# Attention block with an FP8 layer, one core: values and x transposes in mixed blocks, norm values by sums, spread products, four score banks and an end in halves

## What is computed

```python
def _layernorm(x, axis=-1, eps=1e-05):
    m = jnp.mean(x, axis=axis, keepdims=True)
    v = jnp.var(x, axis=axis, keepdims=True)
    return (x - m) / jnp.sqrt(v + eps)
# x: (16, 512, 256)
def attn(x, qkv_w, qkv_b, proj_w, proj_b):        # on _layernorm(x)
    qkv = jnp.einsum('bsd,ed->bse', x, qkv_w) + qkv_b
    # q, k, v: 16 heads of 16 features
    scores = jnp.einsum('bhqe,bhke->bhqk', q, k) * 16 ** -0.5
    out = jnp.einsum('bhqk,bhke->bhqe', jax.nn.softmax(scores, axis=-1), v)
    return jnp.einsum('bsd,ed->bse', out, proj_w) + proj_b
def ffn(x, weight_fp8, bias, input_scale, weight_scale):   # on _layernorm(x)
    x_q = jnp.clip(x / input_scale, -448.0, 448.0).astype(jnp.float8_e4m3fn)
    x_dq = x_q.astype(x.dtype) * input_scale
    return jnp.einsum('bsi,oi->bso', x_dq, weight_fp8 * weight_scale) + bias
x = x + attn(_layernorm(x), ...)
x = x + ffn(_layernorm(x), ...)
```

## Time and profile before

| | |
|---|---|
| median of 3 runs | 969.15 us (968.81 to 969.47) |
| the profiled execution's own time | 968.59 us |
| its span, first to last instruction | 966.8 us |
| TensorE busy | 930.0 us (96%) |
| VectorE, ScalarE, GpSimd busy | 843.8, 656.4, 515.9 us |
| mean granted TensorE clock | 0.974 of full speed |

### The profile page before, as it was taken

One profiled execution on the slowest core, in us unless ns is written; L12 is line 12 of the kernel. 1 busy time (PEld: TensorE's weight loads), 2 busy tenths in 40 slices (PEclk: granted clock), 3 DMA queues, 4 the chain that ended last, 5 costly groups with the idle time before them and its releaser, 6 DMA issues.

```text
span 966.8 us, 16811 instructions
## 1 busy us (share of the span) xinstructions
PE 930.0 (96%) x5847; PEld 439.4 (45%) x5847; DVE 843.8 (87%) x1264; ACT 656.4 (68%) x1209; POOL 515.9 (53%) x528
## 2 busy tenths in 40 slices
PE   7799999999999999999999999999999999999993
PEld 4343444444444454544444444444444454433342
DVE  5678889898999989898998989899898989989846
ACT  3157777777777777767677776767777776776760
POOL 4522428467373847647383754738285573715222
PEclk9769999999999999999999999999999999999996
DMA  6971635438083554717265472817556280731010
GB/s 174 159 91 44 107 52 99 79 62 138 29 142 53 100 78 77 124 40 140 44 115 64 83 116 50 140 34 128 72 74 105 35 136 10 136 42 35 13 45 23
DMA packets 46350, 79.45 MB, mean 82 GB/s; under 512 B 10104, under 2 KB 13304, under 8 KB 46264
## 3 DMA queue, kind: packets, MB, share of 16 engines
q1 hardware_dynamic: 45976, 77.97, 47.1%
q10 hardware_dynamic: 288, 0.39, 0.3%
HBM read 18.42 MB, written 8.39 MB: 28 GB/s over the span
## 4 chain that ended last, share of the span: by engine, by line
PE 92%; DVE 2%; ACT 2%; SPq 1%; DMA 1%; issue 1%; ACTq 0%; POOL 0%; DVEq 0%; POOLq 0%
PE ps_t L551 29%; PE ps_o L591 26%; PE ps_m L426 10%; PE ps_s L570 8%; PE ps_m L475 5%; PE ps_m L499 5%; PE ps_m L531 3%; PE ps_m L412 1%; ACT pt L709 1%; PE ps_s L483 1%; DMA xin<-in_x 1%; SPq L309 1%; PE ps_m L514 1%; DVE mx L874 0%; PE ps_s L692 0%
## 5 line engine op out<-in xcount | busy, mean ns | idle before, releaser
L709 ACT ACTIVATE pt<-ps_t 128x512 f32<-128x512 f32 x1024 | 558.0, 598 | 213.9 <-PE ps_t L551 210.5
L874 DVE TENSOR_REDUCE mx<-ps_s 128x2 f32<-128x1024 f32 x512 | 615.3, 1209 | 57.4 <-PE ps_s L570 53.7
L551 PE MATMUL ps_t<-qs,ks 50*128 50x512 f32 x1024 | 391.9, 455 | 8.2 <-ACT pt L709 7.9
L570 PE MATMUL ps_s<-ks,qs 48*128 48x512 f32 x1024 | 380.7, 463 | 8.0 <-DVE nmax L923 4.1
L551 PEld LDWEIGHTS ps_t<-qs,ks 50*128 50x128 f32 x1024 | 164.0, 185 | 296.3 <-ACT pt L709 214.0
L591 PE MATMUL ps_o<-pt,vt 128*32 128x512 f32 x2048 | 272.6, 605 | 0.0
L1176 POOL TENSOR_TENSOR on<-ot,rden 128x256 f32<-128x256 f32 x63 | 39.3, 624 | 243.2 <-DVE rden L935 243.2
L570 PEld LDWEIGHTS ps_s<-ks,qs 48*128 48x128 f32 x1024 | 158.4, 188 | 18.9 <-issue 11.8
L426 PE MATMUL ps_m<-xnT_p,wqkv_p 128*128 128x512 f32 x360 | 109.9, 428 | 1.0 <-POOL xnT_p L1145 1.0
L1167 POOL TENSOR_TENSOR parts<-parts 128x512 f32<-128x512 f32 x60 | 81.3, 1356 | 4.9
L591 PEld LDWEIGHTS ps_o<-pt,vt 128*32 128x32 f32 x2048 | 40.4, 108 | 86.1 <-issue 85.1
(11 more groups left out here) (113 smaller groups left out, 763.3 us busy)
## 6 DMA issues: line engine op xcount, KB each, us to landing
qs<-parts SPq DMA_DIRECT2D x186, 128.0 KB, 4.6
ks<-parts SPq DMA_DIRECT2D x186, 128.0 KB, 5.4
xin<-in_x SPq DMA_DIRECT2D x16, 512.0 KB, 3.6
xres<-in_x SPq DMA_DIRECT2D x16, 512.0 KB, 5.8
out<-h SPq DMA_DIRECT2D x31, 256.0 KB, 2.1
qs<-nmax SPq DMA_DIRECT2D x256, 4.0 KB
pt<-in_qkv_wT SPq DMA_DIRECT2D x1, 768.0 KB, 5.2
qs<-parts SPq DMA_DIRECT2D x12, 64.0 KB, 3.6
```

The lines of the kernel that those rows point to most:

```text
L551: nc.tensor.matmul(ps_t[:, g, :], ks[par][rows, slot, keys], qs[par][rows, slot, :], start=True, stop=True).then_inc(st_done, 1)
L570: done = nc.tensor.matmul(ps_s[:, s % 2, g, :], qs[par][rows, slot, queries], ks[par][rows, slot, :], start=True, stop=True)
L709: nc.scalar.activation(pt[n % 2][:, w % 2 + 2 * a, w // 2, :], ps_t[:, a, :], ACT.Exp, scale=SCALE).then_inc(exp_done, 1)
L874: dve.tensor_reduce(mx[:, r, :, s % QUARTER], ps_s[:, s % 2, :, :], AX_X, ALU.max).then_inc(max_done, 1)
```

## The change

- Slots 1 to 15: `project_v` and `transpose_x` are replaced by `values_and_x` at the same four steps 20, 22, 24, 26. Each block has six value products (256 columns, one token group) and two transposes of x (128 columns each) into the other half of the same bank. ScalarE reads each block out with two copies of 256 columns instead of one of 512. In slot 15 the blocks have no transposes.
- The norm values become `tensor_reduce` over columns: `mv1` and `mv2` get a third column that holds eps, so that variance + eps is a sum of two columns, and -mean a negated sum of one. The sums of the first norm move from steps 7, 12, 13, 15 with the end at 17 to 5, 7, 10, 12 with the end at 13, and GpSimd's `layernorm_x` goes ahead of `low_oT` of batch u-2.
- Start: x of batch 2 is loaded first in `first_slot` and summed at the end of VectorE's `prepare`, in front of the first maximum; the bias product moves from `ps_o` to `ps_m`, its addition to `prepare`; the transposes of x for batch 1 and five unread matmuls go ahead of the first scores; ScalarE issues the stack of the last keys; SyncE does the first maximum rows ahead of the stack of batch 1. In slot 1 the query and key products of batch 1 stand one at a time in steps 4 to 15 and three at a time in 16 to 19, and unread matmuls in steps 0 to 3 and 8.
- Slot 17: after its first step the odd steps of `scores_t` use the bank pair `ps_s[0]`, so that each waits for the exponential two steps back. The unread matmuls become one in each of the steps 2, 4, 6, 8. The rounding of batch 14 moves from step 8 to 4, the norm's end from 3 to 2, `out_back` from 6 to 9, `copy_oT` from 8 to 12; GpSimd norms first and adds the FP8 layer's bias after the rounding.
- End: `finish` does all value products first and then turns, divides, copies and projects in halves of 256 columns; the normalization of h moves from VectorE to ScalarE (two activations for each of four token groups); 26 unread matmuls stand behind the last projection.

```diff
-LAST_ROUND = 8
+LAST_ROUND = 4
+LAST_END = 2
+LAST_BACK = 9
+LAST_COPY = 12
+FILL_VALUES = 3
+FILL_NORM = 26
-FILL_STEPS = range(3, 12)
+FILL_STEPS = (2, 4, 6, 8)
...
-PROJECT_QK_1 = ((4,), (6,), (8,), (10, 12))
+PROJECT_QK_1 = (range(4, 10), range(10, 16), (16, 17), (18, 19))
-PROJECT_V = (20, 22)
-TRANSPOSE_X = (24, 26)
-TRANSPOSE_X1 = (0, 2)
+VALUES_AND_X = (20, 22, 24, 26)
-LN1_SUM = (7, 12, 13, 15)
-LN1_END = 17
+LN1_SUM = (5, 7, 10, 12)
+LN1_END = 13
+WARM_SCORES = 5
+WARM_STEPS = (1, 1, 1, 1, 0, 0, 0, 0, 3)
...
+        def t_bank(b, s, g):
+            if b == B - 1 and s > HALF_STEPS and s % 2:
+                return ps_s[:, 0, g, :]
+            return ps_t[:, g, :]
...
             def first_slot():
+                load(2, 0)
                 sp.wait_ge(ones, 1)
...
-                for n in (2, 3):
-                    stack(0, 0, n)
-                load(2, 0)
+                stack(0, 0, 2)
...
-                for half in range(2):
-                    project_v(0, half)
+                for i in range(NJ):
+                    project_values(ps_t[:, i // 2, i % 2 * D:(i % 2 + 1) * D], 0, i)
+                pe.wait_ge(low_ready, 4)
+                pe.wait_ge(v_ready, 4)
+                for i in range(WARM_SCORES):
+                    nc.tensor.matmul(ps_s[:, 1, 1, :], wqkv_p[:, 0, 0, 0:P], wqkv_p[:, 0, 0, 0:S], start=True, stop=True)
+                for c in range(NC):
+                    transpose_x(1, c)
...
+            def values_and_x(u, i):
+                take_bank("values_and_x", i, u)
+                project_values(ps_m[:, 0:D], u, i)
+                if u < B - 1:
+                    c, half = i // 2, i % 2
+                    pe.wait_ge(xn_ready, u + 2)
+                    for j in range(2):
+                        last = nc.tensor.transpose(ps_m[:, D + j * P:D + (j + 1) * P],
+                                                   xn[:, 2 * half + j, c * P:(c + 1) * P], ident[:])
+                    last.then_inc(xt_done, 1)
...
+                if b == B - 1 and s == HALF_STEPS + 1:
+                    pe.wait_ge(max_done, STEPS * b + STEPS - 1)
+                elif b == B - 1 and s > HALF_STEPS:
+                    pe.wait_ge(exp_done, 2 * STEPS * b + 2 * s + g - 3)
+                elif past(2 * STEPS * b + 2 * s + g - 1):
                     pe.wait_ge(exp_done, 2 * STEPS * b + 2 * s + g - 1)
...
             def finish(b):
                 values(b, b % 2, UNITS - 1, 0)
+                values(b, b % 2, UNITS - 1, 1)
                 pe.wait_ge(oT_high, NT * b + 1)
...
+                unread(FILL_VALUES)
+                for half in range(2):
+                    pe.wait_ge(oT_high, NT * b + 2 + half)
+                    project_last(1, half, PAIRS[0:3:2])
+                    pe.wait_ge(oT_low, NT * b + 2 + half)
+                    project_last(1, half, PAIRS[1:2]).then_inc(proj_done, 1)
+                unread(FILL_NORM)
...
-                dve.tensor_scalar(nm1[:], mv1[:, :, 0], -1.0, None, ALU.mult).then_inc(ln1_ready, 1)
-                dve.tensor_scalar(ve1[:], mv1[:, :, 1], EPS, None, ALU.add).then_inc(ln1_ready, 1)
+                dve.tensor_reduce(nm1[:], mv1[:, :, 0:1], AX_X, ALU.add, negate=True).then_inc(ln1_ready, 1)
+                dve.tensor_reduce(ve1[:], mv1[:, :, 1:3], AX_X, ALU.add).then_inc(ln1_ready, 1)
...
+                finish_bias()
+                for j in range(NJ):
+                    ln1_sum(2, 0, j)
+                ln1_finish(2)
```

More of the change, by code:

```diff
@@ L354, in slot @@
                     load(u + 2, par)
+                if u == 1:
+                    rows(0, 0, 0)
                 if present(0):
                     stack(u, par, 0)
-                if present(1):
+                if present(1) and u > 1:
                     rows(u - 1, 1 - par, 0)
@@ L401, in take_bank @@
                     pe.wait_ge(y_ready, 2 * before + m + 1)
+                elif last == "bias":
+                    pe.wait_ge(const_v, 3)
                 bank_user[:] = [name, n, b]
             def transpose_x(u, c):
-                first = u == 0
-                bank = ps_t[:, c, :] if first else ps_m[:]
-                if not first:
+                bank = x_bank(u, c)
+                if u > 1:
                     take_bank("transpose_x", c, u)
+                if u == 1 and c == 1:
+                    pe.wait_ge(v_ready, 2)
                 pe.wait_ge(xn_ready, u + 1)
@@ L550, in scores_t @@
                 rows = slice(HALF * g, HALF * g + KM)
-                nc.tensor.matmul(ps_t[:, g, :], ks[par][rows, slot, keys], qs[par][rows, slot, :],
+                nc.tensor.matmul(t_bank(b, s, g), ks[par][rows, slot, keys], qs[par][rows, slot, :],
                                  start=True, stop=True).then_inc(st_done, 1)
@@ L614, in slot @@
                         transpose_max(u - 1, TRANSPOSE_MAX.index(s))
+                    if u == 1 and s < len(WARM_STEPS):
+                        unread(WARM_STEPS[s])
                     for j in range(2):
@@ L635, in slot @@
                     if u == LAST_SLOT and s in FILL_STEPS:
-                        for i in range(2 - s % 2):
-                            nc.tensor.matmul(ps_s[:, 0, i, :], wqkv_p[:, 0, 0, 0:P], wqkv_p[:, 0, 0, 0:S],
-                                             start=True, stop=True)
+                        pe.wait_ge(nmax_split, 8 * (u - 2) + 8)
+                        nc.tensor.matmul(ps_s[:, 1, 0, :], wqkv_p[:, 0, 0, 0:P], wqkv_p[:, 0, 0, 0:S],
+                                         start=True, stop=True)
                     if s % 2:
@@ L651, in bias, with unread @@
                 for t in range(NT):
[L652 removed]
+                    last = nc.tensor.matmul(ps_m[:, 0:D], b_v_rep[:, t, :], wproj[:, t, :],
                                             start=(t == 0), stop=(t == NT - 1))
                 last.then_inc(bias_done, 1)
[L656 to L665 removed]
+            def unread(count):
+                for i in range(count):
+                    nc.tensor.matmul(ps_t[:, 1, :], wqkv_p[:, 0, 0, 0:P], wqkv_p[:, 0, 0, 0:S], start=True, stop=True)
@@ new lines, in project_last @@
+            def project_last(t, half, picks):
+                for j in range(2):
+                    tok = slice((2 * half + j) * P, (2 * half + j + 1) * P)
+                    for pw, px in picks:
+                        last = nc.tensor.matmul(ps_s[:, half, j, 0:D], oT_p[:, px, t, tok], wproj_p[:, pw, t, :],
+                                                start=(t == 0 and (pw, px) == (0, 0)),
+                                                stop=(t == 1 and px == 1))
+                return last
@@ L1054, in finish @@
                 hb = xin[1]
[L1055 to L1063 removed]
+                blocks = [slice(S // 64 * half, S // 64 * (half + 1)) for half in range(2)]
@@ new lines, in finish, with tokens_out, reciprocal @@
+                columns = [slice(S // 2 * half, S // 2 * (half + 1)) for half in range(2)]
+                def tokens_out(half):
+                    dve.wait_ge(pv_done, UNITS * b + UNITS)
+                    dve.wait_ge(on_ready, 4 * b + 3)
+                    dve.transpose(ot[:, blocks[half]].rearrange("p a c -> p (a c)"),
+                                  ps_o[:, columns[half]]).then_inc(ot_ready, 1)
+                def reciprocal(half):
+                    dve.wait_ge(ot_ready, 4 * b + 4 + half)
+                    dve.reciprocal(rden[:, blocks[half]], ot[:, blocks[half], HD]).then_inc(rden_ready, 1)
@@ new lines, in divide, with heads_back @@
+                def divide(half):
+                    dve.wait_ge(rden_ready, 4 * b + 4 + half)
+                    dve.tensor_tensor(on[:, blocks[half], HD:2 * HD], ot[:, blocks[half], 0:HD],
+                                      rden[:, blocks[half]].unsqueeze(2).to_broadcast([P, S // 64, HD]),
+                                      ALU.mult).then_inc(on_ready, 1)
+                def heads_back(half):
+                    dve.wait_ge(on_ready, 4 * b + 4 + half)
+                    dve.wait_ge(oT_low, NT * b + 1)
+                    dve.transpose(oT[:, columns[half]],
+                                  on[:, blocks[half]].rearrange("p a c -> p (a c)")).then_inc(oT_ready, 1)
@@ new lines, in rest @@
+                def rest(half):
+                    dve.wait_ge(oT_high, NT * b + 2 + half)
+                    dve.tensor_tensor(oT_p[:, 1, 1, columns[half]], oT[:, columns[half]],
+                                      oT_p[:, 0, 1, columns[half]].bitcast(F32), ALU.subtract).then_inc(oT_low, 1)
+                tokens_out(0)
+                reciprocal(0)
+                tokens_out(1)
+                divide(0)
+                reciprocal(1)
+                heads_back(0)
+                divide(1)
```

223 lines of the change are left out of this document (113 added, 110 removed).

## The result

The changed kernel takes **943.75 us** (943.17 to 944.86, four runs) against 969.21 us of the kernel before on the same chip: ratio 0.974, 95% interval 0.972 to 0.976. The forecast was 939.2 in a range of 932 to 953. The profiled execution is one of 943.34 us with a span of 941.4.

The account below looks back on a forecast made before the run. TensorE held 92% of the chain, with uneven work and half clock in slot 1. From 968.59: -10.7 (slot 1), -6.5 (slots 2-14), -1.2 (slot 15), -6.6 (slot 17), -5.0 (end) = 938.6; median 0.6 above: 939.2, range 932 to 953.

Parts of the forecast that it names:

- One product a step (0.25 at full, 0.45 at half clock) fits beside a maximum at either level: Slot 1, first half: a product hides beside VectorE's maximum of 1.15 us, helping step 16 come near 42.
- the term of 1.6 us for the clock: Slot 1: 1.6 us added for half clock, the new first half being no denser than 60 to 75% busy.
- rival 2: Half clock stays in slot 1 (+4); 26 end matmuls run at half clock (+4, last pieces +1.3): 948 us; 13%.
- the pauses are gone: Slot 1 and end: argument against lasting half clock, which had followed pauses of 1.9 to 4 us.
- The bound of -6: Start and slot 1: smallest gain, if half clock holds as long as before or the rows come late; forecast -10.7.
- next late: Slot 1: first maximum rows would be late after x's load, but SyncE now issues them before batch 1's stack.
- Rival 1: Mixed blocks gain nothing, as products, transposes and ScalarE's extra copies fill what was saved: +6.5, 946 us; 14%.
- rival 4: Slower: ScalarE's two copies delay each block's scores and exponentials; 0.5 us a pair eats the 30, 4.2 us gives 975; 4%.
- a slack of 1.3 us at step 13: Slots, step 13: 1.3 us of a 2.4 us VectorE hold would be absorbed, thirteen times.
- rival 3: Norm values wait for GpSimd's addition at step 13: 2.4 us less 1.3 of slack, thirteen times, 953 us; 5%.
- The bound of -3.5: Slot 17: smallest gain, if the rounding chain is as late as before (930.1 + 2.6); forecast -6.6.
- the share of the clock: End: last piece 0.6 instead of 1.22 us with 26 unread matmuls keeping full clock, previous piece out of the way: -1.3.

Follow-up runs that it names:

- warm_rows: Changed kernel with one unread matmul also in steps 4-7 and 9-15 of slot 1, first maximum rows queued before x of batch 3: 940.48 us, ratio 0.972.
- warm_two: `warm_rows` with two unread matmuls in each of steps 0-3 of slot 1 and six instead of five before the first scores: 938.17 us, ratio 0.967.
- warm_more: Changed kernel with one unread matmul also in each of steps 4-7 and 9-15 of slot 1: 941.92 us, ratio 0.972.
- unmixed: Changed kernel with twelve value products at steps 20 and 22 and four transposes at 24 and 26 again, copies of 512 columns: 953.48 us, ratio 0.985.
- scalar_norm: Changed kernel with the norm values by tensor_scalar again, the sums' end kept at step 13: 954.76 us, ratio 0.985.
- late_round: Changed kernel with slot 17's norm end at step 3 and rounding at step 8 again: 948.05 us, single run.
- no_end_fill: Changed kernel without the 26 unread matmuls behind the last projection: 948.59 us.

## Why the prediction was right, and where it was wrong

**Slot 1, -5.6 for -10.7: the step that failed** is "One product a step (0.25 at full, 0.45 at half clock) fits beside a maximum at either level". It counted the product alone. Two scores and a product are 1.45 us at half clock (29.88 to 31.33), and the maximum 1.13 to 1.15, so below full clock TensorE becomes the bound, and every step behind 29.6 pays 0.3; step 8, with three unread matmuls, takes 2.74 where `warm_rows` has 2.18, and the four steps from 16 on together 2.6 more than there. With it falls the term of 1.6 us for the clock: slot 1 is 52.1 us in the kernel after and 45.9 in `warm_rows` and `warm_two` at full clock, so the clock costs 6.2. Of the 5.1 us missing, 4.6 are this term; the other 0.5 are in steps and rows that I took a little too short. I had named the danger ("no denser than 60 to 75% busy", rival 2) and given it, together with a half clock where the 26 stand, 13%. Its first half came true: priced at 4 us, it cost 4.6 over the forecast; its second half did not. It was also the usual course and no bad luck: in all eight profiled executions whose first sixteen steps are as in the kernel after, or differ in the norm values alone, the clock fell between 26.9 and 33.2 us. The argument "the pauses are gone" did not hold: between 23.5 and 29.6 TensorE had no wait over 0.20 us and the clock fell all the same. The bound of -6 "if the half clock holds as long as before" was about the result, and shows that the size was in reach.

**The rows of the first maxima** I had as "next late" and judged in time. In the kernel after they are in time, because half clock makes step 16 late by more; at full clock they are 2.00 us late (`warm_more`). I had looked at which engine issues them, not at the 512 KB in front of them.

**Slots 2 to 14, -6.5 for -6.5,** for the reason given: even steps 1.79 (forecast 1.75 to 1.8), pairs 3.45 (3.42 to 3.47), and `unmixed` gives all of it back. Rival 1 falls. That the norm of x had to come earlier was right as well, worth 0.31 a slot. ScalarE's two copies (0.37 and 0.38 us) and two exponentials (1.11) stayed under the pair, so rival 4 falls. Its price was also summed wrongly: 0.5 us over the old mean of 3.57 in 56 pairs are 28 us, but by the forecast's own terms, without the gain of the middle, 22.3 us or 0.4 a pair already eat the whole. The "over 0.4 us of slack" of the maxima at steps 5 to 12 fits the slots measured; a slack of 1.3 us at step 13, on which rival 3's price rested, didn't: 1.25 us of holding cost 0.84 a slot in `scalar_norm`.

**Norm values, 0 for 0,** and the reason was right: the reduction runs beside GpSimd's addition at 0.16 us. What the prediction did not say is what the old form would have cost in the new place. The runs show both: it was harmless at step 17, and it costs 0.84 us a slot at step 13.

**Slots 15 and 16:** -1.3 for -1.2 and 0 for 0; pairs of slot 15 are 3.23, 3.22, 3.34 and 3.22.

**Slot 17, -6.3 for -6.6.** Pairs 2.29 for 2.2: two matmul pairs and an unread matmul at 0.43 each, and value rounds that take the rest; TensorE's own work, not ScalarE, is the larger of the two. The prediction's own terms (two times 0.43, 0.43 and 0.57, 0.43) are 2.29 as well; 2.2 was a slip of the sum. The rounding chain ends 13.3 for 12.9 us into the slot. Both parts are needed: without the second bank pair 4.6 us are lost, with the old place of the rounding 4.9. The bound of -3.5 for a late rounding was too near: 930.1 + 2.6 is 932.7, the forecast itself, and not the 935.8 that -3.5 stands for, and `late_round` leaves 24.91 of 26.23 us, a gain of 1.3, with the rounding only 2.0 us later.

**End, -5.8 for -5.0.** Value products and the turn in halves gave 1.3 and 1.45 (forecast 1.1 and 1.2); from the first residual addition to the last 3.1 (forecast 2.7 for norm and last pieces together). In that, the share of the clock was too small and the norm's too large: `no_end_fill` gives the 26 matmuls 2.1 us where the sum had 1.3, which leaves about 1.0 for ScalarE's norm where it had 1.4. That the sum came near for these two is in part luck, since the two errors cancel. The last share is a difference of two executions, not a run of its own.

**What stays open.** What decides, in one execution and not in the next of the same kernel, whether the clock falls between 26 and 34 us: `warm_rows` ran from 937.4 to 947.8 us. With `warm_two` no run of five had a mean clock under 0.997; of its two additions, the second unread matmul a step and the sixth ahead of the slot, neither was tried alone. Open too is why the 26 unread matmuls at the end held the clock in some executions and not in others.

## What to carry to other kernels

Before a step is called free "at either clock", add up everything that TensorE does in it at half clock and compare the sum with the engine that paces it; where the sum is larger, the clock is part of the critical path, and unread matmuls in the idle time can cost less than nothing. When an instruction of VectorE is moved, look at which GpSimd instruction it will meet there, and whether its form is one that waits for it. And a regained clock uncovers the next late transfer: follow the queue in front of it by bytes, not by number.
